# Two families of transposes moved from TensorE to the DMA crossbar in an attention and mixture-of-experts kernel

## What is computed

```python
h = concatenate([tokens(x), txt], axis=1)            # (64, 82, 256)
# attention, 16 heads of 16, with a relative bias
qkv = layernorm(h) @ w_qkv + b_qkv
attn = softmax(q @ k.T * scale + bias)
out = (attn @ v) @ w_out + b_out                      # heads joined to 256
h = h + out
# experts: the 2048 first tokens, two experts of 8 each
xr = layernorm(h).reshape(T, 256)[tok]                # rows sorted by expert
ye = gelu(xr @ w1A[e].T @ w1B[e]) @ w2A[e].T @ w2B[e] # rank 64, width 1024
h = h + scatter_add(weight * ye)
```

## Time and profile before

| | |
|---|---|
| median of 3 runs | 638.37 us (638.05 to 639.68) |
| the profiled execution | 638.33 us, its span 636.5 us |
| TensorE matmuls busy | 587.2 us, 92% of the span |
| VectorE busy | 492.4 us, 77% |
| ScalarE busy | 368.9 us, 58% |
| POOL busy | 318.2 us, 50% |
| attention, start of scores(0) to scores(63) | 119.34 to 492.09 us |
| pairs of experts | to about 613 us |

### The profile page before, as it was taken

How to read it: one execution, slowest core, us unless ns; L and a number is a source line. 1 busy time by engine, 2 the same in 40 slices (tenths; PEclk the granted TensorE clock), 3 DMA queues, 4 the chain that set the end, 5 groups by cost and what they waited for, 6 DMA issues and landing times.

```text
span 636.5 us, 21150 instructions
## 1 busy us (share of the span) xinstructions
PE 587.2 (92%) x8302; PEld 494.7 (78%) x8302; DVE 492.4 (77%) x1023; ACT 368.9 (58%) x851; POOL 318.2 (50%) x407
## 2 busy tenths in 40 slices
PE   6989988789999999999999999999998899999940
PEld 5778866568888778888898889888887688888830
DVE  2766868689899988999899888988887566666516
ACT  1232134247766666776777667776777756666623
POOL 1520620668978567787744434564223177633330
PEclk9999999889999999999999999999999999999985
DMA  9990004011111117114343232222222033311138
GB/s 304 383 335 1 2 9 159 15 47 30 30 46 36 52 42 210 56 50 121 97 132 103 74 92 65 74 69 68 66 73 81 29 109 101 94 52 50 49 121 321
DMA packets 35629, 61.21 MB, mean 96 GB/s; under 512 B 6156, under 2 KB 21900, under 8 KB 35020
## 3 DMA queue, kind: packets, MB, share of 16 engines
q1 hardware_dynamic: 30732, 49.60, 24.3%
q0 software_dynamic: 4800, 10.27, 5.4%
HBM read 36.18 MB, written 18.00 MB: 85 GB/s over the span
## 4 chain that ended last, share of the span: by engine, by line
PE 67%; DVE 6%; issue 4%; DMA 1%; POOL 1%; ACT 1%; SPq 0%; POOLq 0%; DVEq 0%
PE psQ L1312 11%; PE psQ L1280 10%; PE psS L1303 7%; PE psS L1452 6%; PE psO L1322 6%; PE psO L1467 5%; PE psQ L1290 5%; PE psQ L1346 5%; PE psO L1330 4%; DVE mx L1744 2%; PE psQ L1437 2%; PE psQ L1421 2%; PE psO L1337 2%; PE psQ L1479 1%; PE psQ L1271 1%
## 5 line engine op out<-in xcount | busy, mean ns | idle before, releaser
L1596 ACT ACTIVATE probT<-psQ 82x328 f32<-82x328 f32 x256 | 110.1, 437 | 20.1 <-PE psQ L1312 18.5
L1744 DVE TENSOR_REDUCE mx<-psS 82x8 f32<-82x656 f32 x128 | 106.1, 829 | 11.9 <-PE psS L1303 11.4
L1312 PE MATMUL psQ<-ident_all,prob 82*82 82x82 f32 x1024 | 113.4, 237 | 0.6 <-DVE qk_space L1732 0.6
L1312 PEld LDWEIGHTS psQ<-ident_all,prob 82*82 82x82 f32 x1024 | 89.9, 120 | 28.1 <-issue 6.5
L1746 DVE TENSOR_TENSOR prob<-psS,mx 82x656 f32<-82x656 f32 x128 | 107.1, 837 | 4.4
L1588 ACT ACTIVATE prob<-prob 82x656 f32<-82x656 f32 x128 | 94.9, 742 | 3.2 <-DVE prob L1746 2.5
L1148 POOL TENSOR_TENSOR big<-big,po 128x256 f32<-128x256 f32 x41 | 29.9, 730 | 106.5 <-ACT po L1583 106.1
L1280 PE MATMUL psQ<-hT,wqkv 128*128 128x328 f32 (+10 forms) x320 | 81.0, 387 | 0.0
L1782 DVE COPY qk_space<-ex_weights 64x640 f32 x78 | 40.9, 524 | 35.7 <-PE psQ L1479 33.9
L1566 ACT ACTIVATE oT<-psO 128x328 f32<-128x328 f32 x64 | 28.4, 443 | 64.7 <-PE psO L1322 64.7
L1218 POOL DMA_INDIRECT entry_rows<-yv,slot_entry x39 | 39.3, 1009 | 41.4 <-ACT yv L1634 33.4
(11 more groups left out here) (277 smaller groups left out, 1134.1 us busy)
## 6 DMA issues: line engine op xcount, KB each, us to landing
fused_rows<-in_txt SPq DMA_DIRECT2D x1, 4928.0 KB, 18.1
vv<-vs SPq DMA_DIRECT2D x24, 164.0 KB
big<-in_patches SPq DMA_DIRECT2D x2, 1600.0 KB, 10.7
out<-big SPq DMA_DIRECT2D x25, 128.0 KB, 3.6
big<-entry_rows SPq DMA_DIRECT2D x6, 512.0 KB, 6.7
ex_weights<-in_wa SPq DMA_DIRECT2D x8, 320.0 KB, 3.8
ex_weights<-in_wb SPq DMA_DIRECT2D x8, 320.0 KB, 5.4
normed_rows<-fx SPq DMA_DIRECT2D x16, 128.0 KB
```

The lines of the kernel that those rows point to most:

```text
L1312: mm = te.transpose(bank(("turn", 4 * b + g))[0:T, s * T:s * T + T], prob[:, b % 2, g, s, :], ident_all[0:T, 0:T])
L1596: act.activation(probT[:, b % 2, g, :, :].rearrange("p s t -> p (s t)"), bank(("turn", 4 * b + g))[0:T, 0:4 * T], ACT.Copy).then_inc(S["pr ...
L1744: v.tensor_reduce(mx[:, half, :, :], s4, X, ALU.max).then_inc(S["max_ready"], 1)
```

## The change

It takes `turn_att` and `pair_in` off TensorE. In their place:

- **att.** ScalarE splits `att` into 16-bit planes (`split_att`: low and high halves of each 128 columns, 82 x 512 values of 16 bits), SP issues a transposing DMA of 96 x 512 values from SBUF to SBUF, and ScalarE weaves the planes back into `attT` (`weave_att`, 128 x 328 values), one period after the split. `attT` of a batch is ready one period later, so `project`, the stores of finished tiles, the rows for the experts and the gathers all move by a period or more. `att` has two buffers; `weigh` now waits for VectorE's `normalise` and not for ScalarE's copy.
- **The experts' rows.** ScalarE splits each normalised tile into planes (`split`, 128 x 1024 values of 16 bits) before it is stored; gathers bring rows of planes; SP issues one transposing DMA of 128 x 512 values per gathered tile (`turn_pair`), and `copy_pair` weaves 128 x 1024 values.
- **Moved beside these.** POOL's `add_row` goes from beside `prepare` to a period ahead of its `add_project`; the seven that stood ahead of the loop are gone. One `dots` (three instructions of VectorE) moves from the tokenizer's end into `late(0)`, `late(0)` ahead of `read_qk(1, 0)`, and `token_stats(3..5)` ahead of the tokenizer's last column. `project` of the last two tiles comes after `hidden(1)`, and `result(0)` waits for both copies.

```diff
-                if n >= 16:
+                if 16 <= n < 21:
                     dots(1, n - 14)
...
-            for k in range(3, 6):
-                token_stats(k)
+                    for k in range(3, 6):
+                        token_stats(k)
...
     def projected(b):
-        return [n for n in range(NTL) if last_of[n] == b - 3]
+        return [n for n in range(NTL) if last_of[n] == b - 4]
...
-        uses += earlier[3:4] + ([("pair", 0)] if b == NB - 1 else [])
+        uses += earlier[3:4]
+    uses += [("project", NTL - 3), ("project", NTL - 2), ("low", 1), ("project", NTL - 1)]
...
-        oT = sb("oT", [128, 4, T]); att = sb("att", [T, NH, HD])
-        attT = sb("attT", [128, 2, RA]); rden = sb("rden", [T, NH, 1])
+        oT = sb("oT", [128, 4, T]); att = sb("att", [T, 2, NH, HD])
+
+        att_planes = sb("att_planes", [96, 2, 4, 128], U16); attT_planes = sb("attT_planes", [128, 2, 4, 96], U16)
...
-        gather_at = [max(NN + 12 + j, last_of[n] + 7) for j, n in enumerate(R["xin_tiles"])]
-        R["gathered"] = len([g for g in gather_at if g < NB + 4])
+        gather_at = [max(NN + 12 + j, last_of[n] + 8) for j, n in enumerate(R["xin_tiles"])]
+        R["gathered"] = len([g for g in gather_at if g < NB + 5])
...
+            def turn_pair(p):
+
+                if p < 2:
+                    for k in range(2):
+                        sp.wait_ge(S["fx_sent%d" % k], 16 * NX // 2)
+                elif p < 4:
+                    sp.wait_ge(S["pair_turned%d" % (p % 2)], turned_pairs(p - 2))
+                    for k in range(4):
+                        sp.wait_ge(S["v_in%d" % k], 16 * v_pieces[NB - 4 + k])
+                else:
+                    sp.wait_ge(S["f_xT_ready"], p - 1)
+                for h in halves(p):
+                    j = 2 * p + h
+                    sp.wait_ge(S["xin%d" % (j % 8)], 16 * (j // 8 + 1))
+                    sp.dma_start_transpose(xT_planes(p)[:, h, :, :], row_words(R["xin_tiles"][j % RING])).then_inc(S["pair_turned%d" % (p % 2)], 16)
+
+            def turn_att(b):
+
+                if b >= 2:
+                    sp.wait_ge(S["attT_ready"], b - 1)
+                sp.wait_ge(S["att_split"], b + 1)
+                sp.dma_start_transpose(attT_planes[:, b % 2, :, :], att_planes[:, b % 2, :, :].rearrange("p k n -> p (k n)")).then_inc(S["att_turned%d" % (b % 2)], 16)
+
+            for b in range(-1, NB + 5):
+                if 3 <= b < NB + 2:
+                    turn_att(b - 3)
+                if b == NB + 1:
+                    turn_att(NB - 1)
+                if b in (NB - 8, NB - 6):
+                    turn_pair((b - NB + 8) // 2)
+                if b == NB - 1:
+                    turn_pair(2)
+                    turn_pair(3)
...
-                for n in projected(b - 4):
+                for n in projected(b - 6):
                     if n < NX:
                         sp.wait_ge(S["fx_ready"], n + 1)
-                        sp.dma_start(R["normed"][128 * n:128 * n + 128, :], fx[:, n % 2, :]).then_inc(S["fx_sent%d" % (n % 2)], 16)
+                        sp.dma_start(R["normed"][128 * n:128 * n + 128, :], planes[:, n % 2, :, :].rearrange("p k n -> p (k n)")).then_inc(S["fx_sent%d" % (n % 2)], 16)
+            for p in range(4, NPAIR):
+                turn_pair(p)
...
-                    pool.wait_ge(S["fx_sent%d" % (n % 2)], 16 * (n // 2))
+                    pool.wait_ge(S["fx_ready"], n - 1)
...
-            for n in early:
-                add_row(n)
...
                         prepare(n)
-                        add_row(n)
+                for n in projected(b + 1):
+                    add_row(n)
...
-                te.wait_ge(S["attT_ready"], b)
+                te.wait_ge(S["att_ready"], 2 * b)
...
-            def turn_att(b):
-
-                te.wait_ge(S["att_ready"], b + 1)
-                for c in range(2):
-                    mm = te.transpose(psO[:, c * T:c * T + T], att[:, 8 * c:8 * c + 8, :].rearrange("p h d -> p (h d)"), ident_all[0:T, 0:T])
-                mm.then_inc(S["attT_ps"], 1)
...
-            def pair_in(p):
-
-                for h in halves(p):
-                    j = 2 * p + h
...
-                for h in halves(p):
-                    for c in range(2):
-                        mm = te.transpose(room[:, h, c * 128:c * 128 + 128], H[:, R["xin_tiles"][(2 * p + h) % RING], c * 128:c * 128 + 128], ident_all[:])
-                mm.then_inc(S["f_xT_ps"], 1)
...
-                te.wait_ge(S["f_xT_ready"], min(p + 3, NPAIR))
+                if p == 0:
+                    te.wait_ge(S["psQ_act"], by_act["project", NTL - 1])
...
-                if b >= 2:
-                    turn_att(b - 2)
-            pair_in(0)
             weigh(NB - 2)
             turn(NB - 1, 0)
-            pair_in(1)
             turn(NB - 1, 1)
             turn_back(NB - 2)
             low(0)
             turn(NB - 1, 2)
             turn(NB - 1, 3)
-            turn_att(NB - 2)
             hidden(0)
             weigh(NB - 1)
             low(1)
             turn_back(NB - 1)
-            project(NTL - 2)
-            turn_att(NB - 1)
-            project(NTL - 1)
+            project(NTL - 3)
             down(0)
-            pair_in(2)
             for p in range(1, NPAIR):
                 hidden(p)
+                if p == 1:
+                    project(NTL - 2)
+                    project(NTL - 1)
...
-            def copy_attT(b):
-
-                act.wait_ge(S["attT_ps"], b + 1)
+            def split_att(b):
+
+                act.wait_ge(S["att_ready"], 2 * b + 2)
+                if b >= 2:
+                    act.wait_ge(S["att_turned%d" % (b % 2)], 16 * (b // 2))
+                else:
+                    act.wait_ge(S["planes_set"], 1)
+                act.activation(att_planes[0:T, b % 2, :, :].rearrange("p (c l) n -> p c n l", l=2),
+                               att[:, b % 2, :, :].rearrange("p h e -> p (h e)").bitcast(U16).rearrange("p (c n l) -> p c n l", c=2, l=2),
+                               ACT.Copy).then_inc(S["att_split"], 1)
+
+            def weave_att(b):
+
+                act.wait_ge(S["att_turned%d" % (b % 2)], 16 * (b // 2 + 1))
                 done = (T * b + T - RA + 127) // 128
                 if done > 0:
                     act.wait_ge(S["project_done"], done)
                 for a, lo, size in pieces(T * b, T, RA):
-                    ins = act.activation(attT[:, :, a:a + size], psO[:, 0:2 * T].rearrange("p (c t) -> p c t", c=2)[:, :, lo:lo + size], ACT.Copy)
+                    ins = act.activation(attT_words[:, :, 2 * a:2 * (a + size)].rearrange("p c (t l) -> p c t l", l=2),
+                                         attT_planes[:, b % 2, :, lo:lo + size].rearrange("p (c l) t -> p c t l", l=2), ACT.Copy)
                 ins.then_inc(S["attT_ready"], 1)
...
+            def split(n):
+
+                act.wait_ge(S["fx_normed"], n + 1)
+                if n >= 2:
+                    act.wait_ge(S["fx_sent%d" % (n % 2)], 16 * (n // 2))
+                act.activation(planes[:, n % 2, :, :].rearrange("p (k l) n -> p k n l", l=2), fx_words[:, n % 2, :, :, :], ACT.Copy).then_inc(S["fx_ready"], 1)
+
             def copy_pair(p):
                 n = len(halves(p))
-                act.wait_ge(S["f_xT_ps"], p + 1)
+                act.wait_ge(S["pair_turned%d" % (p % 2)], turned_pairs(p))
                 if p >= 2:
                     act.wait_ge(S["t1_ps"], p - 1)
                 if p == 0:
                     act.wait_ge(S["tok_out0"], 16 * 5)
                     act.wait_ge(S["tok_out1"], 16 * 5)
-                room = bank(("pair", p)).rearrange("p (h n) -> p h n", h=2) if p < 2 else psU
-                act.activation(pair_xT[:, p % 2, 0:n, :, :], room[:, 0:n, 0:256].rearrange("p h (c t) -> p h c t", c=2), ACT.Copy).then_inc(S["f_xT_ready"], 1)
+                act.activation(pair_words[:, p % 2, 0:n, :, :, :].rearrange("p h c t l -> p (h c) t l"),
+                               xT_planes(p)[:, 0:n, :, :].rearrange("p h (c l) t -> p (h c) t l", l=2), ACT.Copy).then_inc(S["f_xT_ready"], 1)
...
+                if b >= 3:
+                    weave_att(b - 3)
                 if b >= 2:
-                    copy_attT(b - 2)
-            copy_pair(0)
+                    split_att(b - 2)
+                for n in projected(b - 5):
+                    if n < NX:
+                        split(n)
+                if b in (NB - 4, NB - 2):
+                    copy_pair((b - NB + 4) // 2)
             copy_oT(NB - 2)
             copy_probT(NB - 1, 0)
-            copy_pair(1)
             copy_probT(NB - 1, 1)
             copy_t1(0)
             copy_probT(NB - 1, 2)
             copy_probT(NB - 1, 3)
-            copy_attT(NB - 2)
+            split_att(NB - 2)
+            weave_att(NB - 3)
             gelu(0, 0)
             copy_oT(NB - 1)
             gelu(0, 1)
             copy_t1(1)
-            copy_project(NTL - 2)
-            copy_attT(NB - 1)
```

(24 more changed lines are left out.)

73 lines of the change are left out of this document (35 added, 38 removed).

## The result

Before 639.02 us (median of 4 runs, 638.05 to 642.66), after **795.85 us** (790.02 to 801.27): ratio 1.246, 95% interval 1.239 to 1.254. I had forecast 622.1 us, 610 to 645: wrong in sign, and far outside the range. The profiled execution of after took 790.95 us, 152.6 more than that of before. Some executions of a kernel take 1.5% or more above its fastest, at a lower granted clock; the ratios and their intervals in this document leave these out, the medians don't.

The account below looks back on a forecast made before the run. TensorE was taken to bound the attention and the experts. Start -3.7, attention -2.6, -6.4 and -1.5, late DMAs +1.5, experts -3.5: -16.2 us from 638.33, so 622.1 us, range 610 to 645.

Parts of the forecast that it names:

- What ScalarE gets: Attention, ScalarE: split_att 0.61 us, weave_att 0.44, attT copy gone, so +0.77 us a period; 1.00 per split of rows.
- Rival C: Attention's first 26 periods: ScalarE becomes the bound, period 6.4 us, 0.3 more than now, +7.8; 640 us in all; chance 12%.
- The TensorE term: Attention, 60 periods: taking turn_att off TensorE gains 2.6 us in the first 26, 6.4 in 29, 1.5 in the last 5.
- L: Attention: landing time of the transposing DMA, taken as 3.6 us (ends 2.5 and 5.4), costing nothing up to 4.25.
- rival D: Attention: transposing DMAs land late, a loop of 6.65 us sets all 60 periods, +48 us; 679 us in all; chance 12%.
- on SP: nothing: Attention, SP queue: transposing DMAs ahead of the values' loads and the stores cost nothing, as their users wait two periods.
- +1.5: Attention: two transposes late behind the two big loads of rows (1408 KB, landing 10.0 us) cost 1.5 us.
- The start: Before the attention: statistics 1.3 us earlier and TensorE's 2.44 us wait for xh gone, together -3.7 us.
- The experts: Expert pairs: POOL paces the first seven at 5.34 us, eleven behind go at 4.89, gaining 4.9; with the transition -3.5 us.
- The transition: Between attention and experts: hidden(1) comes at about 509.7 instead of 512.0, as pair_in(2), turn_att and a project leave its way.
- the last of my signs of a wrong forecast: ScalarE: copies of 16-bit values far from 0.93 us per 1000 columns would show the forecast wrong.
- the one for C: Attention's first stretch: TensorE waiting for probT or oT would show that ScalarE had become the bound.

Follow-up runs that it names:

- the rows' half: Kernel before plus early start and the experts' rows split (new loop order) and turned by DMA, divided sums still on TensorE: 679.62 us, ratio 1.007.
- the better order: The change with both splits reordered, SP issuing the sums' transposing DMA ahead of weights and stores, ScalarE splitting before weaving: 690.53 us, ratio 1.020.

## Why the prediction was wrong

**The step that failed** is in "What ScalarE gets": "copies by columns ... split_att (512) 0.61 ... Bounds: 0.4 if 16-bit columns went at twice the rate, 1.5 at half. I take 0.77, since the instruction counts values." The rows I priced it by all write in a row. The size of the tile was the smaller question; the order of its writes the larger one, and I hadn't read the access pattern for it. With writes in a row 512 values do take 0.62 us, as priced; in the change's order 2.48 and 2.75. So a period got not 0.77 but some 2.7 us more, and 2.75 for a tile of rows instead of 1.00 (a slip besides, there and in the section on the change: that split has 512 values, not 1024). On chip 7 this order alone is 710.5 to 825.2, 115 us of the loss of some 152.

**Rival C** named the mechanism, ScalarE as the bound and TensorE waiting for probT or oT, at 12%. Its price, 0.3 us a period in 26 periods, came from the same 0.77, and it kept 0.9 us a period for waits. Measured were 9.3 us a period in the first stretch: ScalarE's copies 7.6 where I had 5.51 (with twelve splits of rows there, 0.46 a period, where I had read 0.6 off ten periods), and 1.7 of waits, for TensorE above all, which waits for ScalarE in turn and then runs at a lower clock. No run parts the waiting from the clock.

**The TensorE term held, as far as the profiles tell.** Forecast -2.6 - 6.4 - 1.5 = -10.5 us; on chip 7 the 60 periods go from 366.1 with the rows' half alone to 356.3 with the sums' DMAs issued but not waited for, and to 354.6 with them left out: -9.8 and -11.5, one profile each. But the rows' half had cost 5.3 of this first (360.8 to 366.1); I had counted only a smaller gain in the first stretch for it.

**The DMA.** In the first profile L was 2.4 us, 5.3 at most, ScalarE waited 8.5 us in all: rival D did not come true. The figure of the Trainium skill ("VectorE: DVE Perf Modes", The three transpose paths), from which I had worked out an estimated 5.2 us, was too long for this tile here. Yet "on SP: nothing" and "+1.5" for two large loads were wrong, on chip 7 at least: once the splits were cheap, the waits cost 35 us there (356.3 to 391.1), and still 17 in the better order. In the change itself the slow splits hide most of this: ScalarE waits 11.0 us for these DMAs on chip 7, and 34.6 once the splits are in order. Whether the chip of the first result would show as much with cheap splits wasn't run.

**The start** was forecast at -3.7 us, and came out at -5.7 in the first profiles; alone it is worth 1.0 to 1.3%. The mechanism was right, the size small: scores(0) came 1.6 us earlier (forecast 1.3), the 2.44 us of waiting for xh were gone, and the way from there to the scores of batch 3 was 4.1 us shorter (forecast 2.4).

**The experts.** Forecast -3.5 with the transition. The pairs behind POOL's came out as worked out, 4.79 us (4.89 forecast), and POOL paced those ahead of them, at 5.04 to 5.39 (5.34): from hidden(1) to the last hidden 96.3 us against 97.1. The transition, forecast to gain 2.3, lost 9.6: hopping splits and a granted clock of 0.67 stand in it. Which cost what there was not tried; on chip 7, where the change loses 10.1 in it (20.7 to 30.8), the splits' order is 2.6 (30.8 to 28.2) and the wait for the DMAs 5.6 (28.2 to 22.6). The rows' half cost 7.0 us among the experts and 2.1 in the transition on chip 7; by single profiles the moved projections are 6.5 of these 9.1, though the medians don't show it, and the rest is open.

**What the profile would show**: the last of my signs of a wrong forecast, "copies of 16-bit values far from 0.93 us per 1000 columns", and the one for C were what came.

**What stays open**: why the kernel before takes 34 to 38 us more on chips 5 to 7, some 20 of them among the experts on chip 7; why packets stand in the DMA for some 3 us; what the DMAs cost beside the wait; what part of the loss the clock alone has. TensorE's 43 us more of busy time in the 60 periods are an amount, not a share: it waits in the same periods.

## What to carry to other kernels

Price a copy by the order of its writes as well as by its size: on ScalarE 16-bit values written 32 bytes or more apart took 4.7 to 5.4 ns each and those in a row 1.2 to 1.6, with reads that hop by 4, 192 or 256 bytes. So put the outer loop where the destination jumps, and hop in the source. When work moves from a full engine to another in-order engine, ask what stands behind it there. When a DMA enters a loop, try its issue ahead of the bulk transfers on its queue: here that was worth some 16 to 18 of 35 us. And try the side edits of a change alone, since here they held its only gain.

## What the runs showed of the hardware

- ScalarE, 512 16-bit values a row: 0.62 us written in a row, 2.46 to 2.48 us with steps of 256 bytes (82 or 128 partitions), 2.75 right behind another such instruction; steps of 4 bytes, 328 values, 0.57 against 0.50. Reads that hop by 256 bytes, with writes in a row: 1024 values in 1.19 us. VectorE, 512 values with 256-byte steps: 1.55 us.
- A transposing DMA of 96 KB took SP 1.20 us to issue and landed in 2.4 us (2.3 to 5.3) in the first profile; on chip 7 one with 640 KB of weights issued just ahead of it took 5.6 us, and one without 9.6.
- Behind a pause of 3.38 us TensorE was granted 0.50 of its clock, over 3.1 us.
- Thirty-two matmuls of 64x128 that take 2.06 us took 7.6 us (kernel before) and 11 us (rows' half) once in an execution on chip 7, in groups, with nothing that they wait for in the trace.
- The same kernel took 638 us at first and, by the medians, 672 to 676 on chips 5, 6 and 7.
